# Self attention of a decoder layer: queries and keys in tiles of 128 tokens that cross batch borders

## The reference

```python
# x: (8, 224, 512); HEADS 16, DIM_HEAD 64, SOFTCLAMP 50
x = rmsnorm(tokens) * norm_w
q, k, v = x @ Wq, *split(x @ Wkv, 2)
q, k, v = heads(q), heads(k), heads(v)
q = q / max(norm(q), 1e-12) * (q_gamma + 1) * 8     # per token and head
k = k / max(norm(k), 1e-12) * (k_gamma + 1) * 8
sim = tanh(q @ k.T / 50) * 50 / 8                    # within a batch
out = softmax(sim) @ v
x = layernorm(tokens + heads_joined(out) @ Wo)
```

## Time and profile before

| | us |
|---|---|
| median of 3 runs (lowest, highest) | 1798.28 (1795.9, 1801.41) |
| the profiled execution, its own time | 1800.5 |
| its span, first to last instruction | 1798.7 |
| TensorE busy in the span | 1752.8 (97%) |
| VectorE, ScalarE, GpSimd busy | 1402.8, 1184.8, 1110.9 |
| self attention's 16 steps | from about 37 to 551 |
| one step | about 34 |

### The profile page before, as it was taken

How to read it: one execution, slowest core, us unless ns; L and a number is a source line. 1 busy time by engine, 2 the same in 40 slices (tenths; PEclk the granted TensorE clock), 3 DMA queues, 4 the chain that set the end, 5 groups by cost and what they waited for, 6 DMA issues and landing times.

```text
span 1798.7 us, 37447 instructions
## 1 busy us (share of the span) xinstructions
PE 1752.8 (97%) x13942; PEld 1475.8 (82%) x13957; DVE 1402.8 (78%) x3220; ACT 1184.8 (66%) x2691; POOL 1110.9 (62%) x1250
## 2 busy tenths in 40 slices
PE   8999999999998899999999999999999999989997
PEld 7777777777877899999999999899899899975443
DVE  6777778787888677777777788877787777788886
ACT  6878887766765566666666666666566566665774
POOL 3434445654656576786686655588777778652454
PEclk9999999999998999999999999999999999999999
DMA  5222323111105323423422433313314313534553
GB/s 207 77 67 93 100 76 111 50 32 42 52 22 170 123 87 119 143 87 102 153 90 88 146 108 96 113 49 101 109 52 123 96 60 102 129 69 112 146 134 95
DMA packets 141107, 176.82 MB, mean 98 GB/s; under 512 B 63884, under 2 KB 99088, under 8 KB 140928
## 3 DMA queue, kind: packets, MB, share of 16 engines
q1 hardware_dynamic: 122392, 138.15, 25.7%
q0 software_dynamic: 14656, 28.92, 5.9%
q10 hardware_dynamic: 3880, 7.35, 1.4%
HBM read 109.25 MB, written 50.46 MB: 89 GB/s over the span
## 4 chain that ended last, share of the span: by engine, by line
PE 77%; DVE 8%; POOL 5%; ACT 4%; DMA 3%; issue 2%; DVEq 0%; ACTq 0%; POOLq 0%
PE att_ps_T L552 6%; PE att_ps_P L1731 5%; PE att_ps_SA L1755 5%; PE att_ps_P L1719 4%; PE att_ps_SB L612 4%; PE att_ps_P L552 4%; PE att_ps_P L1783 4%; PE att_ps_SB L600 3%; PE att_ps_O L1719 3%; PE att_ps_T L1719 3%; PE att_ps_T L1731 3%; PE att_ps_P L1769 3%; PE att_ps_SA L2465 2%; PE att_ps_O L1731 2%; PE att_ps_P L1794 2%; PE att_ps_T L1783 2%
## 5 line engine op out<-in xcount | busy, mean ns | idle before, releaser
L1537 POOL TENSOR_TENSOR ca_pr<-ca_pr,ca_rec 112x750 f32<-112x750 f32 x256 | 367.0, 1454 | 186.1 <-DVE ca_rec L2017 183.1
L423 POOL TENSOR_TENSOR sa_p_lo<-sa_pr,sa_p_hi 112x448 fp32r<-112x448 f32 x128 | 146.9, 1162 | 210.2 <-ACT sa_p_hi L718 209.4
L1902 ACT ACTIVATE ca_big<-att_ps_P 126x384 fp32r<-126x384 f32 (+1 forms) x254 | 105.3, 449 | 66.1 <-PE att_ps_P L1769 64.6
L1896 ACT ACTIVATE ca_pr<-att_ps_SA,ca_nmax 112x750 f32<-112x750 f32 x128 | 113.7, 889 | 22.1 <-DVE ca_nmax L2013 11.3
L887 DVE RECIPROCAL sa_sums<-sa_sums 128x224 f32<-128x224 f32 x64 | 99.1, 1548 | 33.7 <-ACT sa_sums L727 33.5
L2022 DVE TENSOR_TENSOR ca_big<-att_ps_P,ca_big 126x384 fp32r<-126x384 f32 (+1 forms) x254 | 120.0, 500 | 6.2 <-ACT ca_big L1902 5.9
L2013 DVE TENSOR_REDUCE ca_nmax<-att_ps_SA 112x1 f32<-112x752 f32 x128 | 119.2, 931 | 1.1 <-PE att_ps_SA L1755 1.0
L2013 DVE TENSOR_REDUCE ca_nmax<-att_ps_SB 112x1 f32<-112x752 f32 x128 | 119.2, 931 | 0.0
L1731 PE MATMUL att_ps_P<-ca_w_hi,ca_ct 128*126 128x256 f32 x558 | 114.1, 283 | 1.5 <-DVE ca_q_lo L1996 1.5
L1896 ACT ACTIVATE ca_pr<-att_ps_SB,ca_nmax 112x750 f32<-112x750 f32 x128 | 113.3, 885 | 0.1
L1769 PEld LDWEIGHTS att_ps_P<-att_ident,ca_pr 64*126 64x126 f32 (+1 forms) x1524 | 85.5, 138 | 15.2 <-issue 10.8
(11 more groups left out here) (365 smaller groups left out, 6617.2 us busy)
## 6 DMA issues: line engine op xcount, KB each, us to landing
ct_kept<-ca_ct SPq DMA_DIRECT2D x8, 1134.0 KB, 9.0
ca_ct<-ct_kept POOLq DMA_DIRECT2D x8, 1134.0 KB, 8.0
ct_kept<-ca_ct SPq DMA_DIRECT2D x8, 1116.0 KB, 12.4
ca_ct<-ct_kept POOLq DMA_DIRECT2D x8, 1116.0 KB, 10.2
sa_xin<-in_x_dram SPq DMA_DIRECT2D x16, 448.0 KB, 3.8
xt_kept<-ca_xt SPq DMA_DIRECT2D x8, 896.0 KB, 5.2
ca_xt<-xt_kept POOLq DMA_DIRECT2D x8, 896.0 KB, 5.2
ternary<-ca_stage SPq DMA_DIRECT2D x36, 172.0 KB, 1.9
```

The lines of the kernel that those rows point to most:

```text
L423: pool.tensor_tensor(p_lo[:, h % NB, :], pr[:, h % NB, :], f32(p_hi[:, h % NB, :]), ALU.subtract).then_inc(p_split, 1)
L1537: pool.tensor_tensor(w, w, rec[:, h % PB, c:c + 1].to_broadcast([R, S]), ALU.mult).then_inc(norm_done, 1)
L1896: act.activation(pr[:, h % PB, c, :].rearrange("r (a s) -> r a s", a=2), two_halves(psum[slot]), ACT.Exp, bias=nmax[:, h % PB, c:c + 1], a ...
```

## The change

Queries and keys are projected, normed, scaled and transposed in tiles of 128 tokens, counted through all batches: four batches (PERIOD) have 7 tiles instead of 8. Batches 0, 1 and 2 of a period do two tiles each, batch 3 one (`TILES_OF`). Values stay in tiles of 112. So a projection needs x of the next batch too: x is transposed three batches ahead (AHEAD = 3), into a ring of two batches and 64 columns, and queries and keys go to rings of two batches, in one or two pieces (`RING_PIECES`). XT0 and XT1 keep P0 and P1. With one tile, V0 takes the bank of the absent Q1, and each engine has an order of its own (`WITH_ONE_TILE`): K0 after S3, V0 after O5, V1 after O7, then T0 and T1, and only then Y0. The sum of squares of a row has to be put on another partition for the guard: SP does so with small DMAs in the first 8 batches. `sq` has two places instead of four and `th` two, `p_lo` lies on `pr`. In the start x[1] is loaded into `y` and transposed ahead of Q0, with the split of the first weights (VectorE, ScalarE) before its copies. SP's store of batch 13 moves behind `first_loads`.

```diff
-    AHEAD = 2
+    AHEAD = 3
     LINKS = 1 + RSQRT_LINKS
+    PERIOD = 4
+    XW = 2 * N + HALF
+    TILES_IN = PERIOD * N // P
+    TILE_COLUMNS = [[0, P], [2 * P, 3 * P], [HALF, HALF + P], [2 * P + HALF]]
+    TILES_OF = [[0, 1], [2, 3], [4, 5], [6]]
+    TILES_READY = [[0], [1, 2], [3, 4], [5, 6]]
+    RING_PIECES = [[(0, 0, 2 * P)], [(0, 2 * P, P + HALF), (P + HALF, 0, HALF)], [(0, HALF, 2 * P)], [(0, 2 * P + HALF, P)]]
...
-    norms = psum["O"][0:R, :]
+    norms = psum["O"]
...
-    sq = in_early("sq", [R, 4, DM])
-    xt_hi = in_early("xt_hi", [P, KC, N], F32R)
-    xt_lo = in_early("xt_lo", [P, KC, N], F32R)
-    qs = in_early("qs", [R, 2, GC])
-    ks = in_early("ks", [R, 2, GC])
+    sq = in_early("sq", [P, 2, DM])
+    xt_hi = in_early("xt_hi", [P, KC, XW], F32R)
+    xt_lo = in_early("xt_lo", [P, KC, XW], F32R)
+    qs = in_early("qs", [P, 2, GC])
+    ks = in_early("ks", [P, 2, GC])
...
-    th = in_late("th", [R, NB, 2 * N])
     pr = in_late("pr", [R, NB, 2 * N])
+    in_late.at = at["late"]
+    p_lo = in_late("p_lo", [R, NB, 2 * N], F32R)
     p_hi = in_late("p_hi", [R, NB, 2 * N], F32R)
-    p_lo = in_late("p_lo", [R, NB, 2 * N], F32R)
-    q_hi = in_late("q_hi", [P, NP, N], F32R)
-    q_lo = in_late("q_lo", [P, NP, N], F32R)
-    k_hi = in_late("k_hi", [P, NP, N], F32R)
-    k_lo = in_late("k_lo", [P, NP, N], F32R)
+    q_hi = in_late("q_hi", [P, NP, 2 * N], F32R)
+    q_lo = in_late("q_lo", [P, NP, 2 * N], F32R)
+    k_hi = in_late("k_hi", [P, NP, 2 * N], F32R)
+    k_lo = in_late("k_lo", [P, NP, 2 * N], F32R)
...
+    th = in_late("th", [R, 2, 2 * N])
...
-    UNITS = """XT0 XT1 Q0 K0 Q1 K1 V0 T0 V1 T1 T2 T3""".split()
-    units = [(u, f"P{i % 3}") for i, u in enumerate(UNITS)]
+    UNITS = """Q0 K0 Q1 K1 V0 T0 V1 T1 T2 T3 XT0 XT1""".split()
+    units = [(u, f"P{(i + 2) % 3}") for i, u in enumerate(UNITS)]
...
+    def x_rows(at):
+
+        return y if at(1, 0) == 1 else xin
+
+    def x_loaded(at):
+
+        m = at(1, 0)
+        return (x_in_second, 16) if m == 1 else (x_in, 16 * (m + 1 - (m > 1)))
...
+    def place(u, at):
+
+        if len(tiles(at)) == 1 and u in ("Q1", "V0"):
+            return {"Q1": "V0", "V0": "Q1"}[u]
...
+        return u == "XT0" and number(at) % PERIOD == 2
...
+    def pieces_of(m):
+
+        pieces = []
+        for c in range(2):
+            token, end = m * N + c * R, m * N + c * R + R
+            while token < end:
+                n = min(end, token // P * P + P) - token
+                pieces.append((c, token - m * N - c * R, n, token // P, token % P))
+                token += n
+        return pieces
+
+    def spread_count(m):
+
+        return 16 * sum(len(pieces_of(n)) for n in range(m + 1))
...
+        def spread_squares(m):
+            if m:
+                sp.wait_ge(ss_spread, spread_count(m - 1))
+            for c, r, n, t, row in pieces_of(m):
+                sp.dma_start(tile_ss[row:row + n, t:t + 1], ss[r:r + n, m % 2, c:c + 1]).then_inc(ss_spread, 16)
...
+            if before and number(before) < B:
+                spread_squares(number(before))
...
         load_rows(x[0], None)
+        sp.dma_start(y[:, :, :], x[1].rearrange("(c r) n -> r c n", r=R)).then_inc(x_in_second, 16)
         load_weights(0, range(2))
-        for b in range(1, AHEAD + 1):
-            load_rows(x[b], counter(b - 1, 0, B))
-            if b == 1:
-                load_weights(0, range(2, 4))
-                load_weights(1, range(2))
+        load_rows(x[2], counter(0, 0, B))
+        load_weights(0, range(2, 4))
+        sp.wait_ge(ss_done, 2 * 2)
+        spread_squares(1)
+        load_weights(1, range(2))
+        load_rows(x[3], counter(2, 0, B))
...
-            for b in range(B - AHEAD - 1, B if g + 1 < GROUPS else B - 2):
+            for b in range(B - AHEAD - 1, B if g + 1 < GROUPS else B - 3):
...
         def last_but_one():
+            store(GROUPS - 1, B - 3)
             store(GROUPS - 1, B - 2)
...
+            if u[0] != "V" and c >= len(tiles(at)):
+                return
...
+            if u == "Q1":
+                for t in range(2):
+                    pe.wait_ge(drained[slot[f"XT{t}"]], drained_count(f"XT{t}", lambda per, k: at(per, k) + per))
...
+            if u[0] == "V":
+                rows, col = R, ring_at(at) + c * R
+            else:
+                rows, col = P, TILE_COLUMNS[number(at) % PERIOD][c]
...
+                for c in range(len(tiles(at))):
+                    col = (2 * i + c) * P
+                    mm = pe.transpose(ps(u)[:, col:col + P], t[:, c, p * P:p * P + P], ident[:, :])
...
+        WITH_ONE_TILE = steps("""S1 O0 O1 S2 Q0+ O2 O3 S3 K0+ Q1+ K1+ O4 O5 V0+ O6 O7 V1+ T0+ T1+ Y0 S0+ T2+ Y1 T3+ X+++""")
...
+            if c:
+                act.wait_ge(reduced[0], at(2, i + 1))
+            elif number(at):
+                act.wait_ge(reduced[1], at(2, i - 1))
+            act.activation(sq[:, i, :], ps(u)[:, :], ACT.Square).then_inc(sq_done, 3 if u == "K0" and len(tiles(at)) == 1 else 1)
...
+            for start, to, width in RING_PIECES[number(at) % PERIOD]:
+                q = act.activation(q_hi[:, p, to:to + width], ps(u)[:, start:start + width], ACT.Copy)
+            q.then_inc(t_hi_done, 1)
+            for start, to, width in RING_PIECES[number(at) % PERIOD]:
+                k = act.activation(k_hi[:, p, to:to + width], ps(u)[:, 2 * P + start:2 * P + start + width], ACT.Copy,
+                                   scale=gam[:, 1, g * NP + p:g * NP + p + 1])
+            k.then_inc(t_hi_done, 1)
...
+            if wraps(u, at):
+                act.activation(xt_hi[:, :, 2 * N:XW], x_blocks(u)[:, :, 0, :], ACT.Copy)
...
+        WITH_ONE_TILE = steps("""A2 A3 E2 E3 P2 B0 P3 A4 A5 E4 P4 E5 P5 B1 Q0+ A6 A7 E6 K0+ Q1+ K1+ P6 E7 P7 B2 X+++ W0 L B3 W1 C3
+                                 V0+ W2 V1+ T0+ T1+ A0+ T2+ E0+ A1+ P0+ E1+ P1+ T3+ XT0+++ XT1+++""")
...
-        NEXT_SPLITS = {"K1": (4, range(KC)), "W2": (5, range(3)), "T0": (5, range(3, KC))}
+        NEXT_SPLITS = {"V0": (4, range(KC)), "W2": (5, range(3)), "T0": (5, range(3, KC))}
...
+        def guards(at):
+
+            m = number(at)
+            if m >= B:
+                return
+            ready = TILES_READY[m % PERIOD]
+            of = slice(TILES_IN * (m // PERIOD) + ready[0], TILES_IN * (m // PERIOD) + ready[-1] + 1)
+            dve.wait_ge(ss_spread, spread_count(m))
+            dve.tensor_scalar(guard[:, of], tile_ss[:, of], 1e-24 / DM, 1e-24 * RMS_EPS, ALU.mult, ALU.add).then_inc(guard_done, 1)
...
+        FIRST_PART = """D1 HK0+ N0.0+ N0.1+ N0.2+ N0.3+ N0.4+ N0.5+ N0.6+ N0.7+ N0.8+ N0.9+ N0.10+ N0.11+ Q0+ K0+ HQ1+ HK1+ N1.0+
+                        K1a+ Q1a+ Q1b+ K1b+ I2 D2 I3 U++ V0+ V1+ T0+ T1+ Y0 """
+        WITH_ONE_TILE = [steps(FIRST_PART + """T2+ Y1 G++ T3+ XT0+++ XT1+++ I0+ D0+ I1+ HQ0++"""),
+                         steps(FIRST_PART + """G++ T2+ Y1 F0 T3+ F1 XT0+++ F2 XT1+++ F3 F4 F5 F6 I0+ F7 F8 F9 F10 F11 F12
+                         D0+ F13 HQ0++ I1+""")]
...
-                        if name == "HQ0":
-                            weights_lo(0)
-                            weights_lo(1)
-                            gammas()
-                        elif name == "G":
+                        if name == "G":
                             small_weights()
+                    if isinstance(b, int) and g * B + b + n == 1 and name == "XT0":
+                        weights_lo(0)
+                        weights_lo(1)
+                        gammas()
```

231 lines of the change are left out of this document (147 added, 84 removed).

## The result

The changed kernel takes 1805.46 us (median of 20 runs) and the kernel before, in runs beside it, 1801.22: a ratio of **1.0032, 95% interval 1.0018 to 1.0045**, some 5.8 us slower. The profiled execution took 1804.34, its span 1802.6, where the one before had 1798.7. The forecast was 1793 with a range of 1781 to 1803: wrong in sign, and outside the range. TensorE's busy time went down as meant, from 1752.8 us to 1738.2, but its idle time (span less busy) went up by more, from 45.9 to 64.4.

A forecast was written before the change was run, and what follows sets the result against it. The prediction took TensorE, busy 508 of 511 us in the self attention, as the bound. Its terms, -22.2 - 1.0 + 6.4 + 3.6 + 2.4 + 2.7 + 4.0 - 1.2, gave -5.3 us: 1793 us from 1798.28, range 1781 to 1803.

The forecast's parts named there:

- Removed work: Q and K projections: 8 of 64 fall away, -22.2 us, at an unchanged pitch of 0.232 us; head transposes -1.0 us.
- rival D: Projections with 128 stationary columns are slower: +0.02 us on 672 products, +13 us, 1806 us; chance 0.04.
- The start: Before Q0: transposing x[1] first delays Q0 from 10.79 to 13.2 us, +2.4 us; nothing later in the start swallows it.
- Step 0: First step after the start: +0.4 us by the prediction's terms.
- AHEAD = 3: Prefetch of x in the steps: changes which batch is prefetched, not when in a step; no cost.
- T0's wait: In the four one-tile steps TensorE waits 1.6 us ahead of T0 for V0's low part on VectorE: +6.4 us.
- rival C: In the one-tile steps the clock falls: five waits each bring half-speed work, +8 us, 1801 us; chance 0.12.
- Step 6: One-tile step that also splits the next group's weights: S0 waits for T0's low part, +3.6 us, from 0 to 5.
- Pieces: Copies of queries and keys in two pieces where tiles wrap, extra x copies: +2.7 us, from 0 to 6.
- The switch: Self to cross attention: VectorE's Y0 add waits for batch 13's store, +4.0 us; x wait gone, -1.2 us.
- Rival B: At the switch the store lands 3 us later than thought, with half clock behind: +6 us, 1804 us; chance 0.12.
- Tiny DMAs: SP's two to four small DMAs per batch, eight batches, behind the x load: cost nothing.

The follow-up runs named there:

- e13: The changed kernel with only the start's second guard moved on VectorE, to right behind the scaling of K0: ratio 1.0016 to the kernel before.
- e14: The changed kernel with only the row squares of x[2] moved on ScalarE, from the end of the start to ahead of T0: ratio 1.0012.
- e3: The changed kernel with Y0 ahead of both head transposes T0 and T1 in the one-tile steps: ratio 1.0034.
- e4: The changed kernel with V0's high part (ScalarE) right behind B3 and its low part (VectorE) ahead of the last pair's reciprocal, in one-tile steps: ratio 1.0020.
- e5: The changed kernel with T0 and T1 in exchanged banks and TensorE's order V1 T0 Y0 T1 S0 in one-tile steps: ratio 1.0018.
- e1: The changed kernel with the store of batch 13 back ahead of the cross attention's first loads: ratio 1.0041.
- e2: The changed kernel with both the second guard and the row squares of x[2] moved earlier in the start: ratio 0.9988.
- e6: The changed kernel with GpSimd's last layernorm scaling, which fills y, ahead of the third pair's split in the second group's one-tile steps: ratio 1.0045.
- e7: The changed kernel with GpSimd's last layernorm scaling sooner and the store of batch 13 ahead of the cross attention's first loads: ratio 1.0018.
- e10: The changed kernel with the start's guard and row squares moved, GpSimd's scaling sooner, and batch 13's store ahead of the cross attention's first loads: ratio 0.9979.
- e12: The kernel before the change, with every copy of transposed queries and keys on ScalarE and VectorE made in two pieces of 112 columns: ratio 1.0047.
- e8: The changed kernel with start's guard and row squares moved, T0 and T1 banks exchanged, GpSimd's scaling sooner, and step 6's weight splits later: ratio 1.0013.
- e11: The changed kernel with start's guard and row squares moved, GpSimd's scaling sooner, batch 13's store early, and T0 and T1 banks exchanged: 1792.56 us, ratio 0.9961.
- e15: The kernel of e11 with step 6's splits of the next group's second weight block on ScalarE behind T1 and A0: ratio 0.9953.

## Why the prediction was wrong

It said -5.3 us, and the ratio gives +5.8 (the two profiled executions: +3.8). The steps that failed are the start and step 0: the prediction gave them +2.8 us together and they took +10.4. By its own steps:

- **Removed work, right.** The Q and K projections are in 128 columns and keep their pitch, 0.23 to 0.24 us, as two neighbours of K0 in step 2 show, so rival D is out.

```profile
126.20 0.39 PE L661 MATMUL att_ps_P<-sa_w_hi,sa_xt_hi 128*128 128x512 f32 x1
126.44 0.39 PE L661 MATMUL att_ps_P<-sa_w_lo,sa_xt_hi 128*128 128x512 f32 x1
```

- **The start, mis-sized: +2.4 forecast, +5.7 measured.** Q0 starts at 12.94 (forecast 13.2), so the idle products and the transposes of x[1] cost what was said. The sentence that failed is "Nothing later in the start swallows it, as K1 and T0 wait on chains that shift with it": they shift, and one of them has a new link, the second guard. In the start the sum gave that guard nothing, and in the one-tile steps the 0.2 us of a link; beside GpSimd's split it took 1.8 with the gap behind it. T0's wait grew from 0.68 to 2.25 us, and half clock came behind it: moving the guard gave 1.1 us of wait and 1.6 of clock back (e13).
- **Step 0, missed: +0.4 forecast, +4.65 measured.** The prediction said that AHEAD = 3 changes which batch is prefetched and "not when in a step". In the start it does: the row squares of x[2] were put ahead of the copies at its end. e14 gives 4.06 us for them, 1.2 of it S2's wait and the rest clock. The order of the start was in the diff and was read only for Q0.
- **T0's wait, right in mechanism: 1.6 forecast (its own terms give 127.7 less 126.2, 1.5), 2.2 measured, four times.** VectorE's queue is the one that was added up, with no gap in it from the scaling of Q0 to V0's low part; it ends 0.6 us later against V1 than the sum had it. e3 and e4 show that the queue as a whole is late and not V0's place in it, and e5 that a bank of its own for T0 leaves 1.5 of the 2.2 us, at Y0 and T1.
- **The clock, given to rival C and not to the sum.** C had 0.12. I argued from waits of about 1 us in the start that left the clock at 1.00. Waits of 2.2 us did not always: over the eight kernels with the same order around T0 (the changed kernel, e1, e2, e6, e7, e10, e13, e14), half clock began within 4 us of T0's wait in step 2 in seven, in step 6 in none, in step 10 in five and in step 14 in three, so in 15 of 32. In steps 2 and 10 the wait then cost 3.5 to 3.7 us and not 2.2. In the start, which C did not name, it followed in five of nine. The rule of the Trainium skill (TensorE: Matmul & The Clock Gate, Part 1: The HAM clock gate) that I set beside it, read as I read it, would have left the short waits free; here the measurement decides against that reading. The prediction's "the trace agrees for the short ones" holds for the waits of about 1 us; its own row of 560 to 565 us had half clock behind 1.49 us.
- **Step 6, right in number, in part by luck.** -0.4 forecast, -0.84 measured. The waits for V0's low part and for the keys' low part are there, 2.15 and 1.90 us, but the second was priced at 3.6. The half clock behind it, from about 279 to 284 us, makes up for most of that: without it, in e7, the step is 1.5 us shorter.
- **Pieces, right in size, not all in place.** e12 gives 0.53 us a step. But of the 3.5 us in the eight quiet steps 1.6 are in steps 1, 5 and 9 (0.41, 0.40, 0.78), which have a piece neither of queries and keys nor of x. That they are later is measured; by what, I did not look for.
- **The switch, right in mechanism, mis-sized in the sum.** The text says that O4 should come 4.0 + 1.2 us forward and comes 0.4: by that the store costs 4.8 us, and the sum has 4.0; with 4.8 the whole would be -4.5 us, not -5.3. The repair of it gave 2.9 (e7). In the changed kernel's own times, 6 us later than those of the sum, the store was to land at 555 and O4 to start at 565; the add starts at 554.79 and O4 at 564.24. Rival B, with the store after about 551 in the sum's times, did not happen. But I named the place of the store as the cause. y itself is late (e1), the loads ahead are long (e6), and only both repairs together give the 3 us (e7).
- **Tiny DMAs, nothing.** No wait for them in the steady steps.

Start and step 0 together are 7.6 us of the 8.3 between the table's two sums. Steps 2 and 10 are 1.6 more and the quiet steps 1.5; step 7 gave 1.6 back, step 6 and the last stretch 0.4 each. Of the 7.6, up to 3 us are clock that other kernels with the same start did not lose (22.2 against 20.6 us in the start, 39.8 against 38.5 in step 0), so part of the miss is the draw of this one profile.

Not settled: e2_start gains 8 us by its ratio, but 1.7 by the spans of the two profiled executions (1800.9 and 1802.6). The intervals allow 3 to 13 us. Where the difference goes beyond the switch was not looked for.

## What to carry to other kernels

Count the start as a stretch of its own. There every engine's order is strict, nothing is ahead to cover with, and an operation of 0.15 us put into a chain costs what it takes beside its neighbours there, and the same line in the trace of before can show that price (here 1.02 us); a change that saves in 4 of 16 steps can lose all of it once. Price a TensorE wait like these, 2.2 us among dense products, at the wait and, as a second term with a chance of its own, half clock behind it: here in 15 of 32 cases, at 1.5 us in step 2 and 1.3 in step 10. Where a transfer must land before something is reused, ask two things, when its data is ready and how many bytes are ahead of it in its queue; repairing one of them alone can show nothing.

## What the runs showed of the hardware that I had not expected

- **A two-column operation of VectorE took 1.29 us when it began just behind one of GpSimd's on SBUF, in all nine kernels that have it there, and 0.16 us in the six that have it elsewhere (e2, e8, e10, e11, e13, e15).** The kernel before has the same at 1.02 us. Nothing in the row names the cause; one sees it only with the two engines side by side.
- **The same wait draws half clock in one kernel and none in another.** T0's wait in step 10 is 2.19 to 2.21 us in eight kernels with the same TensorE order around it. In five of them (e1, e2, e6, e7, e10) half clock followed, and step 10 was 1.3 us longer than in the three without (the changed kernel, e13, e14). In step 14 it is the other way round: half clock in these three and in none of the five. What decides it was not found. Two of them, windows of the changed kernel and of e1_store_early:

```profile
412.00:416.00 4.00, 4.00 (x28) 2.93 (x27) 1.01 (x4) 1.15 (x6) 2.24 (x3) 1.00 0.23 67
```

```profile
412.00:416.00 4.00, 3.45 (x13) 2.67 (x14) 2.28 (x8) 0.96 (x4) 3.62 (x5) 0.71 0.00 0
```

So a repair that moves everything earlier by some microseconds can gain or lose 1.3 us in a step that it does not touch, as e2_start did (4.2 of its 5.5 us were left after step 10).
- **A store of 448 KB landed 10.6 to 12 us after the issue of the last of the big loads ahead of it, whether it was issued 0.5 or 4 us behind them.**
